# Sums over fetched rows in a graph kernel: the one-hot becomes the stationary operand, 18 node tiles of 19 runs

## What is computed

```python
deg = segment_sum(ones_like(edge_src), edge_dst, n); dinv = deg ** -0.5
norm = dinv[edge_src] * dinv[edge_dst]
root = einsum('nf,kfg->nkg', x, root_w)
for t in range(3):
    h = einsum('nf,kfg->nkg', x, init_w) if t == 0 else einsum('nkf,kfg->nkg', out, w)
    msg = h[edge_src] * norm[:, None, None]
    h = segment_sum(msg, edge_dst, n)
    out = relu(h + root + b)
```

## Time and profile before

| | us |
|---|---|
| median of three timed runs (lowest, highest) | 3352.11 (3344.53, 3356.41) |
| the profiled execution, its own time | 3317.19 |
| its span, first to last instruction | 3315.3 |
| PE busy in the span | 3133.6 (95%) |
| POOL busy in the span | 834.1 (25%) |
| pass 0, 1022.5 to 1471.3 | 448.8 |
| pass 1, 1471.3 to 1951.6 | 480.3 |

### The profile page before, as it was taken

One profiled execution on the slowest core, in us unless ns is written; L12 is line 12 of the kernel. 1 busy time (PEld: TensorE's weight loads), 2 busy tenths in 40 slices (PEclk: granted clock), 3 DMA queues, 4 the chain that ended last, 5 costly groups with the idle time before them and its releaser, 6 DMA issues. The chain is left out here.

```text
span 3315.3 us, 51940 instructions
## 1 busy us (share of the span) xinstructions
PE 3133.6 (95%) x18657; PEld 1902.1 (57%) x18658; DVE 1341.3 (40%) x5159; ACT 771.9 (23%) x1620; POOL 834.1 (25%) x808
## 2 busy tenths in 40 slices
PE   7897999999999999998999999999999999929998
PEld 4464666665655666655666655555555556616775
DVE  7846778777762222222222212222221004624443
ACT  3444555555540000000000000000000002513333
POOL 3100000000003666626566610000000000654555
PEclk9896999999999999999999999999999999959999
DMA  7221554654738777766777768888889996436886
GB/s 192 80 66 60 185 212 161 239 216 161 247 162 314 243 242 242 255 218 213 239 231 249 236 221 282 290 291 292 291 291 321 303 302 195 148 129 176 203 199 138
DMA packets 244598, 723.87 MB, mean 218 GB/s; under 512 B 35343, under 2 KB 153347, under 8 KB 242354
## 3 DMA queue, kind: packets, MB, share of 16 engines
q1 hardware_dynamic: 181140, 609.25, 54.9%
q0 software_dynamic: 48256, 99.18, 10.8%
q10 hardware_dynamic: 15006, 12.82, 1.4%
HBM read 542.84 MB, written 189.35 MB: 221 GB/s over the span
## 5 line engine op out<-in xcount | busy, mean ns | idle before, releaser
L1831 PE MATMUL first_sum<-stage,split 128*128 128x448 f16 x4704 | 949.7, 354 | 1.9 <-DMA split<-fresh_d 1.9
L1831 PE MATMUL first_sum<-stage,other 128*128 128x448 f16 x3332 | 687.2, 353 | 0.0
L1831 PEld LDWEIGHTS first_sum<-stage,split 128*128 128x128 f16 x4704 | 450.1, 98 | 374.3 <-issue 5.3
L1781 PE MATMUL first_sum<-stage,other 128*128 128x448 f16 x2744 | 648.9, 354 | 0.2 <-ACT stage L1323 0.2
L1308 POOL DMA_INDIRECT stage<-fresh_d,lane_two x272 | 261.5, 961 | 1088.1 <-DMA fresh_d<-split 933.4
L1831 PEld LDWEIGHTS first_sum<-stage,other 128*128 128x128 f16 x3332 | 315.1, 98 | 244.7 <-issue 1.4
L1323 ACT ACTIVATE stage<-group_ps 128x392 f16<-128x392 f32 x784 | 385.6, 497 | 295.4 <-PE group_ps L1770 292.1
L1467 DVE TENSOR_SCALAR place<-iota_col,rel 128x196 f16<-128x196 f16 x1568 | 349.3, 266 | 0.0
L1781 PEld LDWEIGHTS first_sum<-stage,other 128*128 128x128 f16 x2744 | 253.7, 98 | 139.4 <-issue 2.0
L1308 POOL DMA_INDIRECT stage<-later_d,lane_two x272 | 261.6, 962 | 217.7 <-PE group_ps L1873 122.5
L1464 DVE TENSOR_TENSOR lanes<-iota_two,lane_two 128x256 f16<-128x256 f16 x784 | 225.7, 288 | 80.8 <-PE group_ps L1770 68.9
(11 more groups left out here) (383 smaller groups left out, 3019.6 us busy)
## 6 DMA issues: line engine op xcount, KB each, us to landing
stage<-adj_d SPq DMA_DIRECT2D x434, 784.0 KB, 4.2
adj_d<-stage SPq DMA_DIRECT2D x14, 5488.0 KB, 18.4
row_d<-slow_rows SPq DMA_DIRECT2D x12, 3340.5 KB, 29.9
other<-pack_d SPq DMA_DIRECT2D x38, 898.0 KB, 4.8
slot_rows<-row_d SPq DMA_DIRECT2D x38, 393.0 KB, 5.6
stage<-root_d SPq DMA_DIRECT2D x28, 448.0 KB, 7.0
xnT_d<-other SPq DMA_DIRECT2D x14, 448.0 KB, 4.2
split<-root_d SPq DMA_DIRECT2D x14, 448.0 KB, 3.9
```

The costliest lines, as they stand in the source:

```text
L1781: m = mm(acc[b][k][:, 0:WIN], other[:, h, half, k * P:(k + 1) * P], stage[b][:, h, :], start=(h == 0 and half == 0), stop=(h == TILES - 1 ...
L1831: m = mm(acc[b][k][:, 0:WIN], side(t)[:, h, part, k * P:(k + 1) * P], ring[:, i, r, :], start=(h == 0 and part == 0), stop=(h == TILES - 1 ...
```

## The change

`SPARSE = 18` node tiles of 128 (2304 nodes, 5 windows and 64 columns) are summed from fetched rows, each from 19 runs, so there are 342 gathers a pass instead of 272. The first dense window starts at column 64 of window 5 and streams 384 columns; nine dense windows are left, 441 tiles a pass. A run is now one matmul: the one-hot of 128 targets (128 columns) is stationary, and the 512 values of the fetched rows stream, which gives nodes on partitions and the two halves' sums side by side in one bank. ScalarE scales the high half out (`sums_high`), VectorE adds the low half (`sums_low`), PE turns the 128 x 256 sums by two transposes against the identity (`sums_turned`), and VectorE adds the root and clips (`sums_hidden`). There is one bank for the sums, and the next tile's first run waits for `sums_low`; the course leaves three tiles between. Inside a node tile the runs stand one each dense tile, from x = 30 on; the last is at 408. The lists are laid out for three gathers of 126 starts (`listed_at`). The largest node tile of these inputs needs 2230 of the 2432 places.

```diff
-UNITS = 4
-STRIP = 112
-STRIPS = WIN // STRIP
-STRIP_GROUPS = STRIP // G
-CHUNK = 17
-LISTED = UNITS * STRIPS * CHUNK
+SPARSE = 18
+FIRST_DENSE = SPARSE * P // WIN
+OVERLAP = SPARSE * P - FIRST_DENSE * WIN
+CHUNK = 19
+ABREAST = P // SPARSE
+GATHERS = -(-CHUNK // ABREAST)
+LISTED = SPARSE * CHUNK
 TAKEN = (range(0, 3), range(3, SUB))
...
-    BEGIN, TAIL, LEAD, SETTLE, AFTER, APART = 28, 22, 10, 6, 8, 2
+    BEGIN, TAIL, LEAD, GAP = 30, 30, 10, 3
+    TURN, ADD, PROJECT, AFTER, APART = 3, 5, 9, 8, 2
 
     def __init__(self, windows):
         self.tiles = windows * TILES
-        self.chunk_at = [self.BEGIN + c * (self.tiles - self.BEGIN - self.TAIL) // LISTED for c in range(LISTED)]
-        self.strip_end = [self.chunk_at[(s + 1) * CHUNK - 1] + 2 for s in range(UNITS * STRIPS)]
-        self.row_at = {}
-        for pair in range(UNITS // 2):
-            for u in range(SUB):
-                self.row_at[(pair, u)] = self.strip_end[pair * 2 * STRIPS + -(-(u + 1) * P // STRIP) - 1] + self.SETTLE
+        span = self.tiles - self.BEGIN - self.TAIL
+        self.chunk_at = []
+        for s in range(SPARSE):
+            first, after = (self.BEGIN + n * span // SPARSE for n in (s, s + 1))
+            self.chunk_at += [first + c * (after - first - self.GAP) // (CHUNK - 1) for c in range(CHUNK)]
+        self.summed_at = [self.chunk_at[(s + 1) * CHUNK - 1] for s in range(SPARSE)]
+        self.row_at = {s: at + self.PROJECT for s, at in enumerate(self.summed_at)}
         for n in range(windows):
-            for place, u in enumerate(TAKEN[n % 2]):
-                self.row_at[((n + UNITS) // 2, u)] = (n + 1) * TILES + self.AFTER + self.APART * place
...
     def piece_after(self, x):
-        return x // PT + PIECES + 1
+        return x // PT + PIECES - 1
+
...
+def listed_at(s, c):
+    return c // ABREAST * P + c % ABREAST * SPARSE + s
...
+        HELD = 4
...
-        rin_s = space.take(2, WIN)
-        dinv_s = space.take(WIN)
-        hid_s = space.take(2, 2 * WIN)
+        rin_s = space.take(2, 2, P)
+        rows_s = space.take(2, D)
+        hid_s = space.take(HELD, 2, P)
...
-                def unit_roots(t, unit):
-                    cols = slice(unit * WIN, (unit + 1) * WIN)
...
-                def stored_at(pair):
-                    at = courses[0].piece_after(courses[0].row_at[(pair, SUB - 1)])
-                    return max(at, (ND - 1) * PIECES) if pair < UNITS // 2 else at
...
+                def sparse_roots(t, s):
+                    S = t * SPARSE + s
+                    if S >= 2:
+                        sp.wait_ge(s_v, S - 1)
+                    sp.dma_start(rin_s[:, s % 2, :, :], root1_d.rearrange("p (k n) -> p k n", k=2)[:, :, s * P:(s + 1) * P]).then_inc(s_in[s % 2], 16)
+
+                def roots_at(t, s):
+                    return 2 + s if s < 2 else courses[t].piece_after(courses[t].summed_at[s - 1])
+
+                def some_out(n):
+                    if n < PARTED:
+                        sp.wait_ge(s_rows, n + 1)
                     else:
-                        sp.wait_ge(d_rows, pair - UNITS // 2 + 1)
-                    js = slice(pair * SUB, (pair + 1) * SUB)
+                        sp.wait_ge(d_rows, n - PARTED + 1)
+                    js = slice(SOME[n][0], SOME[n][-1] + 1)
                     sp.dma_start(tables_d[1][:, js, :, :], other[:, js, :, :]).then_inc(t_rows, 16)
...
+                def stored_at(n):
+                    at = courses[0].piece_after(courses[0].row_at[SOME[n][-1]] + 2)
+                    return max(at, (ND - 1) * PIECES) if n < PARTED else at
 
                 for t in range(2):
                     for m in range(ND * PIECES):
                         n, i = divmod(m, PIECES)
                         M = t * ND * PIECES + m
+                        for some in range(len(SOME)):
+                            if M == stored_at(some):
+                                some_out(some)
                         if M >= PIECES:
...
                             pool.wait_ge(s_row[g % RING], 16 * (g // RING))
+                        at = listed_at(*divmod(c, CHUNK))
                         nc.gpsimd.indirect_dma_start(got[:, g % RING, :, :].rearrange("p s c -> p (s c)"), None, tables_d[t].rearrange("p j s c -> (p j) (s c)"),
-                                                     bass.IndirectOffsetOnAxis(ap=tab_row[:, c:c + 1], axis=0)).then_inc(s_row[g % RING], 16)
+                                                     bass.IndirectOffsetOnAxis(ap=tab_row[:, at:at + 1], axis=0)).then_inc(s_row[g % RING], 16)
...
+                def sums_high(t, s):
+                    S = t * SPARSE + s
+                    if S >= 2:
+                        act.wait_ge(s_pt, S - 1)
+                    act.wait_ge(s_used, t * LISTED + (s + 1) * CHUNK)
+                    nc.scalar.activation(rows_s[:, S % 2, :], group_ps[0][:, 0:D], ACT.Copy, scale=dinv[:, s:s + 1]).then_inc(s_hi, 1)
...
-                def strip_finish(t, s):
-                    S, at = t * PARTED + s, s % STRIPS * STRIP
-                    one = hid_s[:, :, s % (2 * STRIPS) * STRIP:(s % (2 * STRIPS) + 1) * STRIP]
-                    ps = group_ps[S % 2][:, :].rearrange("p (k c) -> p k c", k=2)[:, :, 0:STRIP]
-                    if s % STRIPS == 0:
-                        dve.wait_ge(s_in, 32 * (t * UNITS + s // STRIPS + 1))
-                    dve.wait_ge(s_used, t * LISTED + (s + 1) * CHUNK)
-                    nc.vector.tensor_tensor(one, ps, dinv_s[:, at:at + STRIP].unsqueeze(1).broadcast_to([P, 2, STRIP]), ALU.mult).then_inc(s_ev, 1)
-                    dve.wait_ge(s_ev, S + 1)
-                    nc.vector.tensor_tensor(one, one, rin_s[:, :, at:at + STRIP], ALU.add).then_inc(s_v, 1)
+                def sums_low(t, s):
+                    S = t * SPARSE + s
+                    one = rows_s[:, S % 2, :]
+                    dve.wait_ge(s_hi, S + 1)
+                    nc.vector.scalar_tensor_tensor(one, group_ps[0][:, D:2 * D], dinv[:, s:s + 1], one, ALU.mult, ALU.add).then_inc(s_ev, 1)
+
+                def sums_hidden(t, s):
+                    S = t * SPARSE + s
+                    one = hid_s[:, S % HELD, :, :]
+                    dve.wait_ge(s_in[S % 2], 16 * (S // 2 + 1))
+                    dve.wait_ge(s_pt, S + 1)
+                    nc.vector.tensor_tensor(one, group_ps[1][:, 0:D].rearrange("p (k n) -> p k n", k=2), rin_s[:, S % 2, :, :], ALU.add).then_inc(s_v, 1)
                     dve.wait_ge(s_v, S + 1)
...
                 def one_hot(t, c):
                     g = t * LISTED + c
+                    at = listed_at(*divmod(c, CHUNK))
...
-                    nc.vector.tensor_scalar(hot[:, g % HOTS, :], iota_col[:, 0:STRIP], tab_key[:, c:c + 1], None, ALU.is_equal).then_inc(s_hot, 1)
-
...
                             one_hot(t, c)
-                        for s in course.strips(x):
-                            strip_finish(t, s)
+                        for s in course.summed(x - 1):
+                            sums_low(t, s)
+                        for s in course.summed(x - Course.ADD):
+                            sums_hidden(t, s)
...
-                def tile_sums(t, b, h, i, r):
+                def tile_sums(t, b, h, i, r, lo=0):
                     for k in range(BLOCKS[t]):
                         for part in range(2):
-                            m = mm(acc[b][k][:, 0:WIN], side(t)[:, h, part, k * P:(k + 1) * P], ring[:, i, r, :],
+                            m = mm(acc[b][k][:, lo:WIN], side(t)[:, h, part, k * P:(k + 1) * P], ring[:, i, r, lo:WIN],
...
-                    S = t * PARTED + s
-                    if first == 0 and S >= 2:
-                        pe.wait_ge(s_ev, S - 1)
+                    S = t * SPARSE + s
+                    if first == 0 and S >= 1:
+                        pe.wait_ge(s_ev, S)
                     pe.wait_ge(s_hot, g + 1)
                     pe.wait_ge(s_row[g % RING], 16 * (g // RING + 1))
+                    mm(group_ps[0][:, :], hot[:, g % HOTS, :], got[:, g % RING, :, :].rearrange("p s c -> p (s c)"), start=(first == 0),
+                       stop=(first == CHUNK - 1), skip_group_check=True).then_inc(s_used, 1)
+
+                def sums_turned(t, s):
+                    S = t * SPARSE + s
+                    pe.wait_ge(s_ev, S + 1)
+                    if S >= 1:
+                        pe.wait_ge(s_v, S)
                     for k in range(2):
-                        for part in range(2):
-                            m = mm(group_ps[S % 2][:, k * D:k * D + STRIP], got[:, g % RING, part, k * P:(k + 1) * P], hot[:, g % HOTS, :],
-                                   start=(first == 0 and k == 0 and part == 0), stop=(first == CHUNK - 1 and part == 1), skip_group_check=True)
-                    m.then_inc(s_used, 1)
+                        m = nc.tensor.transpose(group_ps[1][:, k * P:(k + 1) * P], rows_s[:, S % 2, k * P:(k + 1) * P], ident[:, :])
+                    m.then_inc(s_pt, 1)
```

(4 more changed lines are left out.)

342 lines of the change are left out of this document (173 added, 169 removed).

## The result

The changed kernel took **3523.68 us** (median of 4 runs, 3521.31 to 3531.92) where the kernel before took 3348.69 beside it (3344.53 to 3356.41): ratio **1.052**, 95% interval 1.050 to 1.055. The sign of the prediction was right; the step was 175 us instead of 26.5, and outside the range. Pass 0 lasts 544.5 us (before 448.8, forecast 474.1), pass 1 556.8 (before 480.3, forecast 481.5): together 172 us more.

The account below looks back on a forecast made before the run. PE bounds the kernel before; GpSimd's gather issue, 1.266 us each, would bind both changed passes. +25.3 us in pass 0 and +1.2 in pass 1 give +26.5, so 3378 us, range 3358 to 3408.

Parts of the forecast that it names:

- Tensor work: PE's own sum in the two passes falls to 434.7 us (14.1 less) and 456.3 us (24.0 less).
- The single bank at nothing: At node-tile borders, emptying the one sum bank (about 1 us, against a 2.3 us gap) hides behind the gathers' delay.
- Gathers become the bound, ring or no ring: In both passes POOL needs 24.1 us a node tile where PE wants 21.6; eight buffers give only a lead.
- the prediction's own sum: Pass time is the last gather's start, 3.9 us landing, then PE's closing work (25.2 or 25.7): 474.1 and 481.5 us.
- 333 and 341 steps of 1.266 us, and POOL's waits for PE gone: POOL issues back to back from 23.3 us (pass 0) and 20.2 us (pass 1); its 243 us of waits vanish.
- The rows behind it: Gathers at pass heads, eight 1.257 us apart and 30 averaging 1.27, were taken to show POOL's floor.
- Head of pass 1: POOL's first gather starts 20.2 us in instead of 31.0, and PE's 9.9 us wait almost goes.
- Rival one: Gathers keep up in both passes, so PE's own sums hold: -37 us, 3315 us; chance 0.08.
- Rival two: PE's standing still in the passes lowers its clock to 1.2 GHz for a quarter of the time: +89 us, 3441; chance 0.07.
- Rival three: Gathers bind, but slack in PE's work in these passes hides most of it: +8 us, 3360; chance 0.10.

Follow-up runs that it names:

- half_gathers: The changed kernel with only every second run's rows fetched, 171 gathers a pass instead of 342: 3312 us against 3370 for the kernel before.
- free_paced_four: The changed kernel with no run reading the fetched rows, GpSimd never waiting for PE, and a pause of about 0.5 us after every fourth gather: 3313 us.
- two_banks: The changed kernel with each run as two 256-column matmuls into the same columns, node tiles taking two banks in turn: 3547 us, ratio 1.052 to the kernel before.
- ring14: The changed kernel with fourteen buffers for fetched rows instead of eight: 3558 us, ratio 1.056 to the kernel before.
- share14: The changed kernel's new form with the old share, 14 node tiles and 266 gathers a pass: 3367 us against 3370 for the kernel before, ratio 0.999.
- paced_four: The changed kernel with a GpSimd pause of about 0.5 us after every fourth gather: 3430 us, ratio 1.033 to the kernel before.

## Why the prediction was right or wrong

- *Tensor work.* Right. PE's own passes, read where gathers don't hold it (half_gathers, free_paced_four), are 428 to 429 and 449 to 453 us; forecast 434.7 and 456.3. The run was priced at 0.216 us and takes 0.21; the turns were priced twice too high (0.22 us a pair, so 3.6 us a pass too much).
- *The single bank at nothing.* Right: two_banks and half_gathers show no cost of its own, though the profile after names VectorE as the one PE waits for. I had listed that as a sign of being wrong; the wait only moved when the bank was doubled.
- *Gathers become the bound, ring or no ring.* Right in kind; ring14 changed nothing. Put in the measured start of the last gather (514.7 us into pass 0, 523.1 into pass 1) and the prediction's own sum gives 514.7 + 3.9 + 25.3 = 543.9 and 523.1 + 3.9 + 25.7 = 552.7 us, where 544.5 and 556.8 were measured.
- *333 and 341 steps of 1.266 us, and POOL's waits for PE gone.* **This step failed.** The sum lets GpSimd issue back to back to the end of the pass; it has no term for the way back of a used buffer. The price of an issue held (1.26 us where nothing blocks). What came instead were 82 us of waits for used buffers in pass 0 and 77 in pass 1, for counts that the waiting engine saw 4.06 and 2.77 us (median) after the run had started. So the last gathers started 70 and 71 us later than forecast, 141 of the 146 us by which the two passes exceed the forecast. That the lateness comes with the number of gathers is shown by share14 on one chip; what delays the signals stays open.
- *The rows behind it.* "1.257 us is POOL's floor for a gather" rests on rows of eight and thirty gathers in a trace of the other kind of chip than the one of after. Whether the forecast would hold on chip 15 wasn't run. The nearest is paced_four there: with its 1.38 us the prediction's sum gives 23.3 + 333 x 1.38 + 29.2 = 512.0 and 20.2 + 341 x 1.38 + 29.6 = 520.4 us, and 521.8 and 530.5 were measured, 10 us more in each.
- *Head of pass 1.* The first gather starts 17.8 us in, 20.2 forecast.
- *Rival one* (gathers keep up, and with it the Trainium skill, "DMA: Bandwidth & Descriptors", "Issuing engines are not separate DMA queues"): did not happen. In the rows of before the issue of a gather, 1.25 us, is indeed shorter than its landing, 4.0, as the page says it usually is; that alone hides nothing. half_gathers shows that the rival's sum was sound for a kernel that needs a gather every 2.2 us. *Rival two* (the clock): 0.94 against 0.99 over a pass, and PE's prices stayed as forecast, so the loss lies inside the waits. *Rival three*: no. The 35 us between the profiled and the timed runs, which it spread evenly over PE's work, lie almost all in one stretch behind the passes.

No case of mine allowed for one engine slowing another without a shared buffer or wait between them. The trace of before had a hint of it: five signals up to 2.8 us late at the heads of the passes.

## What to carry to other kernels

A short row of instructions that only start work elsewhere shows what issuing costs, not what hundreds of them do to the other engines. Where a plan rests on such a rate, measure it over hundreds in a row, beside the other engines, before building on it. When an engine's waits name a partner that was itself waiting, compare when signals were sent with when they were seen. Here asking for less, 270 gathers a pass, was the only variant that came out ahead of the kernel before, by 0.6% on its chip. And before two kernels are compared, look whether they ran on the same chip: code that the change doesn't touch, timed in both traces, tells at once, and here it would have shown that the breaks were compared across two kinds of chip.

## What the runs showed of the hardware

- Gathers of 128 rows issued without a break: step 1.25 us for some 215 us, then 1.40 us, alike for rows of 1 KB (chip 14) and of 512 bytes (chip 11). Their packets kept up with the issue: 170 gathers' worth of 171 issued.
- Meanwhile PE, which had no wait on them, fell within 20 us to one matmul every 2.80 us, at a granted clock of 0.50 (1.2 GHz). With a mean step of 1.38 us it ran undisturbed at 1.00 (2.4 GHz), but on chip 15.
- With 342 gathers a pass PE's matmuls kept their recorded pace (0.21 us a run) while their signals reached ScalarE, VectorE and GpSimd up to 8.9 us late. What delays the signals was not shown.
- Chips differ: a stretch with 98 indirect DMAs took 158 us in the trace of before and on chip 15, and 190 to 196 in the trace of after and on chips 3, 11, 12 and 14.
